# A one-core ViT block on Trainium2: the first projection in high and low parts with its loads split, and three routed tiles picked from parts that GpSimd makes

## The reference

```python
h = tok(x, W, b, cls_token, pos_enc)          # patches @ W.T + b, class token, + pos_enc
h = h + attn(layernorm(h), ...)               # a * cumsum(K @ W) @ U.T, Z terms, @ Wo.T
h = h + ffn(layernorm(h), ...)

logits = xf @ w_router + b_router
topv, topi = top_k(softmax(logits), 2)
pos = cumsum(one_hot(e_flat, 8), axis=0)[arange(n * 2), e_flat] - 1
keep = pos < cap                              # cap = 185
buf = zeros((8, cap, d)).at[e_flat, posc].add(where(keep, xf[tok], 0))
hid = gelu(einsum('ecd,edf->ecf', buf, w1) + b1)
out = einsum('ecf,efd->ecd', hid, w2) + b2
# every token gets back the weighted mean of its kept experts' rows
```

## Time and profile before

| | us |
|---|---|
| median of 3 runs | 159.71 |
| lowest and highest | 159.04, 161.41 |
| profiled execution, first to last instruction (span) | 157.9 |
| PE busy in it | 148.0 |
| DVE, ACT, POOL busy in it | 105.5, 82.8, 50.9 |

### The profile page before, as it was taken

How to read it: one execution, slowest core, us unless ns; L and a number is a source line. 1 busy time by engine, 2 the same in 40 slices (tenths; PEclk the granted TensorE clock), 3 DMA queues, 4 the chain that set the end, 5 groups by cost and what they waited for, 6 DMA issues and landing times.

```text
span 157.9 us, 2961 instructions
## 1 busy us (share of the span) xinstructions
PE 148.0 (94%) x982; PEld 138.4 (88%) x982; DVE 105.5 (67%) x330; ACT 82.8 (52%) x210; POOL 50.9 (32%) x55
## 2 busy tenths in 40 slices
PE   7999999999999979999999999999999999999950
PEld 6548999899789768899799899999999999999940
DVE  0074994769887898981396859669486694785710
ACT  3222754644317998857066557474682665737100
POOL 6001200505530000005437167084371661604361
PEclk9999999999999999999999999999999999999995
DMA  5999960079000345301499897888868978600422
GB/s 169 406 420 435 394 230 0 0 243 338 5 0 22 138 163 184 116 0 28 97 349 292 272 269 194 269 192 307 269 130 270 262 250 264 131 7 0 48 25 23
DMA packets 16978, 28.46 MB, mean 180 GB/s; under 512 B 1133, under 2 KB 13591, under 8 KB 16585
## 3 DMA queue, kind: packets, MB, share of 16 engines
q1 hardware_dynamic: 14505, 25.49, 46.6%
q0 software_dynamic: 2464, 2.86, 10.6%
HBM read 24.21 MB, written 4.14 MB: 180 GB/s over the span
## 4 chain that ended last, share of the span: by engine, by line
PE 65%; DMA 11%; DVE 7%; ACT 6%; issue 3%; POOL 3%; SPq 1%; POOLq 1%; DVEq 0%
PE ps L1298 20%; PE ps L1333 10%; PE ps L1132 6%; PE ps L1223 6%; DMA w_even<-w 5%; DMA first_t<-first 4%; PE ps L1335 4%; PE ps L1240 3%; ACT xn L556 2%; PE ps L1165 2%; PE ps L1343 2%; PE ps L1310 2%; DMA rows_in<-xrows,src_row 2%; PE ps L1261 2%; ACT xn L565 2%
## 5 line engine op out<-in xcount | busy, mean ns | idle before, releaser
L497 POOL DMA_INDIRECT out_rows<-out_s,dst_row x16 | 23.8, 1485 | 38.4 <-ACT out_s L682 32.1
L658 ACT ACTIVATE first_t<-ps,b_cur 128x186 f32<-128x186 f32 x64 | 23.0, 413 | 23.5 <-PE ps L1298 22.0
L1333 PE MATMUL ps<-hid_hl,split 128*128 128x372 f32 x96 | 29.1, 369 | 0.0
L1335 PE MATMUL ps<-hid_hl,split 128*128 128x186 f32 x96 | 23.9, 249 | 0.0
L1298 PE MATMUL ps<-first_t,patch_t 128*128 128x186 f32 x128 | 21.7, 322 | 0.1
L977 DVE CAST hid_hl<-first_t 128x372 fp32r<-128x372 f32 x28 | 10.7, 383 | 15.9 <-ACT first_t L658 15.9
L1298 PEld LDWEIGHTS ps<-first_t,patch_t 128*128 128x128 f32 x128 | 20.1, 190 | 0.4 <-issue 0.4
L482 POOL DMA_INDIRECT rows_in<-xrows,src_row x14 | 15.6, 1113 | 11.0 <-DVE src_row L945 7.1
L1298 PE MATMUL ps<-first_t,w_even 128*128 128x186 f32 x112 | 18.9, 321 | 0.0
L522 ACT ACTIVATE split<-patch_t 128x512 fp32r<-128x512 f32 (+2 forms) x28 | 14.4, 577 | 8.1 <-DMA patch_t<-patches 5.7
L1335 PEld LDWEIGHTS ps<-hid_hl,split 128*128 128x128 f32 x96 | 18.3, 191 | 0.0
(11 more groups left out here) (179 smaller groups left out, 263.2 us busy)
## 6 DMA issues: line engine op xcount, KB each, us to landing
w_even<-w SPq DMA_DIRECT2D x8, 1024.0 KB, 5.7
patch_t<-w SPq DMA_DIRECT2D x8, 1024.0 KB, 5.5
att<-attn SPq DMA_DIRECT2D x1, 1280.0 KB, 9.4
patch_t<-patches SPq DMA_DIRECT2D x1, 1188.0 KB, 14.0
patch_t<-patches SPq DMA_DIRECT2D x1, 1080.0 KB, 11.5
first_t<-first SPq DMA_DIRECT2D x1, 978.0 KB, 7.0
out_rows<-h SPq DMA_DIRECT2D x2, 384.0 KB, 2.5
xrows<-xn SPq DMA_DIRECT2D x2, 384.0 KB, 3.5
```

Source lines behind the costliest of these rows:

```text
L497: pool.indirect_dma_start(out=out[:, :], out_offset=bass.IndirectOffsetOnAxis(ap=dst_row[0:SIZES[s], c:c + 1], axis=0), in_=out_s[q][0:SIZ ...
L658: ins = act.activation(hid[:, f, :], bank(pair)[:, (f % 2) * SL:(f % 2 + 1) * SL], ACT.Gelu, bias=b1_cur[q][:, f:f + 1])
L1333: pe.matmul(dst[:, 0:2 * SL], w2_h[q][:, f, cols], hid_hl[:, f].rearrange("p a s -> p (a s)"), start=f == 0, stop=False)
L1335: ins = pe.matmul(dst[:, 0:SL], w2_l[q][:, f, cols], hid_hl[:, f, 0], start=False, stop=f == KF - 1)
```

## The change

- The first projection's loads are six, one for each slice, with `vecs` behind the second. Slices 0 and 1 stay plain fp32; for 2 to 5 ACT makes high parts of weights and patches and DVE the low parts, and PE makes three f32r products of each, the high product of a slice ahead of the low ones of the slice before.
- `att` is loaded in two pieces: output matrices (384 KB) in front of the second projection's patches, the rest behind. Unit `mac` moves behind the second projection, and its steps on ACT too; `m_high` now stands in front of `xn_high`.
- The rows of tiles 6, 7 and 8 are split by POOL into f32r parts; their one-hots are written as f32r; PE picks them by two f32r products (high and low) for each half. Tile 9 is picked before them. `keep2` of group E moves in front of `rows2` of C.
- POOL makes `at_p` for tiles 7 and 8, the product with the tiles' first rows, and the product with the first part of the weights. DVE keeps the rest.
- `look_up` stands in front of the last up pair of expert 0 instead of behind it. ACT loads the Gelu table behind the half copy.

```diff
+PICK_PARTED = (6, 7, 8)
+PLACES = [*range(6), 9, *PICK_PARTED]
+BY_POOL = (7, 8)
...
-PIECES = [(0, 1), (1, 3), (3, KP)]
+PLAIN = 2
...
-        UNITS = [("proj", A, 0), ("mac", 0, 2), ("uw", 0, 1), ("norm1", A, 0), ("proj", B_, 3), ("norm1", B_, 3),
+        UNITS = [("proj", A, 0), ("uw", 0, 2), ("norm1", A, 0), ("proj", B_, 3), ("mac", 0, 1), ("norm1", B_, 3),
...
-        ACT_ORDER = [("mac", 0), ("root1", A), ("norm1", A), ("xn_high", A), ("m_high", 0), ("root1", B_), ("norm1", B_),
+        ACT_ORDER = [("root1", A), ("norm1", A), ("mac", 0), ("m_high", 0), ("xn_high", A), ("root1", B_), ("norm1", B_),
...
-                     ("rows2", B_), ("squares2", C), ("root2", C), ("rows2", C), ("keep2", E), ("rows2", E), ("keep2", C)]
+                     ("rows2", B_), ("squares2", C), ("root2", C), ("keep2", E), ("rows2", C), ("rows2", E), ("keep2", C)]
...
-            for i, (a, b) in enumerate(PIECES):
+            for k in range(KP):
                 w = D + FIRST
-                sp.dma_start(first_t[:, a:b].rearrange("p k d -> p (k d)"), first[:, a * w:b * w]).then_inc(first_in[i], 16)
-            sp.dma_start(vecs[:, :], vectors).then_inc(vec_in, 16)
-            sp.dma_start(att[:, :], attn).then_inc(attn_in, 16)
+                sp.dma_start(first_t[:, k], first[:, k * w:(k + 1) * w]).then_inc(first_in[k], 16)
+                if k == PLAIN - 1:
+                    sp.dma_start(vecs[:, :], vectors).then_inc(vec_in, 16)
+            sp.dma_start(att[:, 0:A_U.stop], attn[:, 0:A_U.stop]).then_inc(uw_in, 16)
             for g in range(1, len(PATCHES)):
                 c0, c1 = patch_cols(g)
                 sp.dma_start(patch_t[:, c0:c1], patches[:, c0:c1]).then_inc(patch_in[g], 16)
                 if g == 1:
+                    sp.dma_start(att[:, A_U.stop:], attn[:, A_U.stop:]).then_inc(attn_in, 16)
                     sp.dma_start(cst[:, :], const).then_inc(const_in, 16)
...
+            for i, t in enumerate(PICK_PARTED):
+                if t == GROUPS[C][0]:
+                    pool.wait_ge(row_made, 1)
+                elif t < GROUPS[E][0]:
+                    done(pool, ("rows2", C))
+                else:
+                    pool.wait_ge(row_made, 2)
+                pool.tensor_copy(pick_h[:, i], xn[:, t]).then_inc(row_high, 1)
+                pool.wait_ge(row_high, i + 1)
+                pool.tensor_tensor(pick_l[:, i], xn[:, t], pick_h[:, i], ALU.subtract).then_inc(row_split, 1)
+
+            pool.wait_ge(slots_fixed, 1)
+            for t in BY_POOL:
+                for k in range(2):
+                    pool.tensor_scalar(at_p[:, t, k], iota_slot[:, 0:ST], slot_p[:, t, k:k + 1], None, ALU.is_equal
+                                       ).then_inc(pool_marked, 1)
+            pool.wait_ge(places_known, 1)
+            for c in range(1, ID_SUM):
+                start = ids.rearrange("p (t c a b) -> p t c a b", c=ID_SUM, a=1, b=1)[:, :, c]
+                pool.tensor_tensor(marks[:, :, :, 1 + c], at_q, start.broadcast_to((TT, NT, 2, SC)), ALU.mult
+                                   ).then_inc(pool_marked, 1)
+            pool.wait_ge(first_part, 1)
+            pool.tensor_tensor(marks[:, :, :, ID_PARTS], at_q, spread(parts[:, :, :, 0], NT, SC), ALU.mult
+                               ).then_inc(pool_marked, 1)
+
...
-            for i, (a, b) in enumerate(PIECES):
-                act.wait_ge(first_in[i], 16)
-                copy(tok_h[:, a:b], tok_wt[:, a:b]).then_inc(tok_high, 1)
+            for k in range(PLAIN, KP):
+                act.wait_ge(first_in[k], 16)
+                copy(tok_h[:, k], tok_wt[:, k])
+                copy(patch_h[:, k, 0:FIRST], first_t[:, k, D:]).then_inc(first_high, 1)
+            for k in range(PLAIN):
+                act.wait_ge(first_in[k], 16)
+            copy(tok_h[:, 0:PLAIN], tok_wt[:, 0:PLAIN]).then_inc(tok_high, 1)
...
+            patches_high(SPLIT[1], inside=INSIDE + 1)
...
-                    patches_high(SPLIT[1], inside=INSIDE + 1)
...
-            act.activation(idle[:, :], eps_col[0:1], ACT.Gelu)
-
             act.wait_ge(picked, KD)
             copy(buf_t[0][:, 1:], pick_slot[:, 1:]).then_inc(half_ready, 1)
+
+            act.activation(idle[:, :], eps_col[0:1], ACT.Gelu)
...
-            for i, (a, b) in enumerate(PIECES):
-                dve.wait_ge(tok_high, i + 1)
-                dve.tensor_tensor(tok_l[:, a:b], tok_wt[:, a:b], tok_h[:, a:b], ALU.subtract).then_inc(tok_split, 1)
+            for k in range(PLAIN, KP):
+                dve.wait_ge(first_high, k - PLAIN + 1)
+                dve.tensor_tensor(patch_l[:, k, 0:FIRST], first_t[:, k, D:], patch_h[:, k, 0:FIRST], ALU.subtract)
+                dve.tensor_tensor(tok_l[:, k], tok_wt[:, k], tok_h[:, k], ALU.subtract).then_inc(first_split, 1)
+            dve.wait_ge(tok_high, 1)
+            dve.tensor_tensor(tok_l[:, 0:PLAIN], tok_wt[:, 0:PLAIN], tok_h[:, 0:PLAIN], ALU.subtract).then_inc(tok_split, 1)
...
-                for t in range(t0, t0 + n):
-                    dve.tensor_scalar(onehot[:, t], iota_slot[:, 1:SL + 1], place0[:, t:t + 1], None, ALU.is_equal
+                for t in PLACES[t0:t0 + n]:
+                    dst = onehot_r[:, PICK_PARTED.index(t)] if t in PICK_PARTED else onehot[:, t]
+                    dve.tensor_scalar(dst, iota_slot[:, 1:SL + 1], place0[:, t:t + 1], None, ALU.is_equal
...
-            n = marked(dve.tensor_tensor(slot_p[:, :, :], slot_p[:, :, :], lost[:, :, :], ALU.add))
+            dve.tensor_tensor(slot_p[:, :, :], slot_p[:, :, :], lost[:, :, :], ALU.add).then_inc(slots_fixed, 1)
             behind(m)
             m = marked(dve.tensor_tensor(got[:, :], weight[:, :, 0], weight[:, :, 1], ALU.add))
-            behind(n)
+            dve.wait_ge(slots_fixed, 1)
             dve.tensor_tensor(at_q[:, :, :, :], grid(iota_slot[:, 0:SC], NT, 2, SC), spread(slot_q[:, :, :], NT, SC), ALU.is_equal
                               ).then_inc(places_known, 1)
             behind(m)
             m = marked(dve.scalar_tensor_tensor(got[:, :], every[:, :], 1e-6, got[:, :], ALU.mult, ALU.max))
             take_in(0, 0, first=True)
-            find_slots(0, 2)
+            find_slots(0, 1)
             behind(m)
             m = marked(dve.reciprocal(got[:, :], got[:, :]))
-            dve.wait_ge(places_known, 1)
-            for c in range(1, ID_SUM):
-                start = ids.rearrange("p (t c a b) -> p t c a b", c=ID_SUM, a=1, b=1)[:, :, c]
-                dve.tensor_tensor(marks[:, :, :, 1 + c], at_q, start.broadcast_to((TT, NT, 2, SC)), ALU.mult)
...
+            dve.tensor_copy(parts[:, :, :, 0], weight[:, :, :]).then_inc(first_part, 1)
...
             m = rest_after(1)
-            find_slots(7, 9)
+            find_slots(6, BY_POOL[0])
             behind(m)
             m = part_of(2)
-            find_slots(9, NT)
+            find_slots(BY_POOL[-1] + 1, NT)
             behind(m)
-            for k in range(2):
-                ins = dve.tensor_tensor(marks[:, :, k, ID_PARTS:],
-                                        at_q[:, :, k].rearrange("p t (a q) -> p t a q", a=1).broadcast_to((TT, NT, PARTS, SC)),
-                                        parts[:, :, k].rearrange("p t (c a) -> p t c a", a=1).broadcast_to((TT, NT, PARTS, SC)),
-                                        ALU.mult)
+            dve.wait_ge(places_known, 1)
+            for c in range(1, PARTS):
+                ins = dve.tensor_tensor(marks[:, :, :, ID_PARTS + c], at_q, spread(parts[:, :, :, c], NT, SC), ALU.mult)
             ins.then_inc(marks_ready, 1)
...
+                pe.wait_ge(pool_marked, 2 * len(BY_POOL) + ID_SUM)
...
-                pick_tiles(range(t0 - HELD, t0), range(KD))
-                for k in range(KD):
-                    pick_tiles(range(t0, t0 + c), [k]).then_inc(picked, 1)
+                pick_tiles([*range(t0 - HELD, t0), *(t for t in PLACES[t0:] if t not in PICK_PARTED)], range(KD))
+                for i, t in enumerate(PICK_PARTED):
+                    pe.wait_ge(onehot_ready, PLACES.index(t) + 1)
+                    pe.wait_ge(row_high, i + 1)
+                    for k in range(KD):
+                        pe.matmul(pick_slot[:, k, :], pick_h[:, i, k * 128:(k + 1) * 128], onehot_r[:, i, :],
+                                  start=False, stop=False)
+                    pe.wait_ge(row_split, i + 1)
+                    for k in range(KD):
+                        ins = pe.matmul(pick_slot[:, k, :], pick_l[:, i, k * 128:(k + 1) * 128], onehot_r[:, i, :],
+                                        start=False, stop=t == PICK_PARTED[-1])
+                        if t == PICK_PARTED[-1]:
+                            ins.then_inc(picked, 1)
...
-                        for i, (a, b) in enumerate(PIECES):
-                            pe.wait_ge(first_in[i], 16)
-                            for d in range(KD):
-                                for k in range(a, b):
```

(32 more changed lines are left out.)

43 lines of the change are left out of this document (24 added, 19 removed).

## The result

The changed kernel took **161.79 us** (median of 4 runs, 160.66 to 162.31), the kernel before beside it 159.38 (4 runs): a ratio of 1.0145, 95% interval 1.0104 to 1.0186. That is 2.4 us slower in the medians (2.3 by the ratio), where 0.8 us faster was forecast; the time lies above the range given (157.4 to 161.3). The profiled execution had a span of 160.1 us, against 157.9 before.

The account below looks back on a forecast made before the run. PE, busy 94% of the span, was taken as the bound, with DVE's serial chain deciding in the routing. Terms -1.1 - 0.25 - 0.4 + 1.0 = -0.75 us gave span 157.15; plus 1.8, rounded to 158.9 us, range 157.4 to 161.3.

Parts of the forecast that it names:

- the front: First projection through second: split loads and f32r slices gain 1.1 us, moved `mac` and earlier `m_high` 0.25; shift 1.35.
- POOL beside DVE: Routing: POOL's added operations hold up DVE's short steps in three waits of 0.33 us, 1.0 us lost.
- rival 2: Routing, `is_one` to `marks`: POOL holds up DVE throughout, 2.0 us before the copy, 1.3 at look-up; 161.2 us, chance 0.25.
- Marks and look-up: Expert 0's look-up: marks 1.05 us earlier if POOL costs nothing; look-up loses nothing, earlier row numbers and loads gain 0.4.
- `m_l` wait: PE's 0.26 us wait for POOL at 31.62 goes, as ACT runs `m_high` before `xn_high`; gain 0.25 us.
- Picks: Routing, three tiles in f32r: 0.7 us less PE work, counted at nothing because PE is not late there.
- The clock: Clock falling in PE's longer gap, together with rival 2, was the only way above 162.9 us; chance 0.05.

Follow-up runs that it names:

- bystander: Kernel before with spare products, plus POOL's three copies and three subtractions, whose results nothing reads; half copies wait for the last: 160.92 us, ratio 1.0091.
- changed kernel with spare products: Changed kernel plus products nobody reads, filling PE's two gaps ahead of the first pick: 161.73 us, ratio 1.0138.
- control: Kernel before plus products nobody reads, filling PE's two gaps ahead of the first pick: 159.82 us, ratio 1.0013.
- front bridged: Kernel before with only the changed front, plus unread spare products in PE's two gaps ahead of the first pick: 159.91 us, ratio 1.0035.
- Picks back: Changed kernel with all picks in fp32 again and POOL's six splitting steps out; marks shared, look-up early: 161.07 us, ratio 1.0076.
- routing-only: Kernel before with only the changed picks, marks and look-up; front as before: 161.97 us, ratio 1.0123.
- only the marks shared: Changed kernel with spare products, look-up late, picks in fp32 without POOL's six steps; POOL keeps its share of marks: 159.94 us, ratio 1.0016.
- the look-up early: Kernel before with spare products, only the look-up moved one up pair earlier, nothing on POOL: 160.15 us, ratio 1.0027.

## Why the prediction was wrong

By stretches the forecast was -1.35 for the front, +1.0 up to the first up product and -0.4 behind it; the traces show -0.47, +1.51 and +1.23. The differences are 0.9, 0.5 and 1.6 us; of the 0.5, some 0.3 us is the clock's fall in that trace.

**POOL beside DVE** was sized right up to the copy: 1.0 us forecast, 0.95 to 0.99 in the traces of bystander and changed kernel with spare products, in three waits, as forecast. Which three was partly wrong. `is_one` was named and waited, `chosen` hardly did (0.27), and `at_q` took 0.49 us as before; the others were `below` and the one-hots, which the forecast had at its upper end only. The one-hots are of a kind that the rows had not shown, with a single large operand in SBUF: 1.47 us for four against 1.00. The Trainium skill (SBUF — State Buffer, section "SBUF: two separate sides") has it that a DVE operation in a 2-port mode is locked out by a GpSimd one too. The traces show the one-hots held, as that would have it, but not in which mode they ran. The price of rival 2, 2.0 us before the copy, did not come; its side of the result did.

**The step that failed is "Marks and look-up"**, forecast as nothing lost and 0.4 us gained. It took the marks to be ready 1.05 us earlier, less two waits, because DVE had less to do. They were ready 71.66 - 66.50 = 5.16 us after the copy, before 70.46 - 65.47 = 4.99: no earlier at all. POOL's `at_p` took 0.66 us each, not 0.25, so its two products came late, at 68.67 and 69.36, onto DVE's last steps, 0.89 instead of 0.35 and 0.70 instead of 0.17. PE then stood 0.70 us. The 0.4 us counted as a gain for earlier row numbers became a loss of 0.66. The row numbers did let expert 2's first matrix be issued 0.37 us earlier against the first up product (11.11 us behind it, 11.48 before), but the load in the chain of waits is the second matrix, which also waits for the end of expert 0 on PE: it started 12.60 us behind the first up product instead of 12.08, and took 8.33 us instead of 7.57, the latter for reasons that stay open. With the look-up moved back both losses went in the traces, 1.17 us in the medians. So the step is wrong by 1.6 us in all, twice the net gain that was forecast.

**The front** was mis-sized: 1.35 us forecast, 0.47 at `slots` (0). The first projection ended at 12.64, not 11.85, because ACT got its slices at 6.41 and 8.61 and PE's eight plain records took 0.55 us each instead of the 0.355 reckoned with, and the second projection started at 14.60, not 13.95; the patches came at 13.04, not 12.45. Of the `m_l` wait of 0.26 us, DVE's `h_t` gave 0.18 back. The baseline also varies: the control's trace has the same fp32 projection ending at 3.86 + 8.51 = 12.37, with no wait for a load, 0.6 us earlier than in the trace from which the gain was reckoned. In three other traces these 24 records, with no wait either, took 9.53 to 9.91 us and ended at 13.44 to 13.64. So not only loads vary there but PE's records. With the split front the first projection ended at 12.29 to 12.64 in seven of nine traces, and later (13.53 and 15.83) where ACT had its slices late. By these traces the split front is worth about 1 us where PE's early fp32 records are slow, and nothing where they are quick; in the medians nothing is left: front bridged 159.91, control 159.82.

**Picks**: counted at nothing, and that held. With the spare products PE stood 1.32 us for the copy in the changed kernel, where it stood 0.26 in the control.

**The clock** had 0.05 as a cause beyond rival 2. It fell, and in that trace the stretch to the first up is 0.30 us longer than without it (10.53 against 10.23). Taking the fall away left the time where it was: the table under "Picks back" shows that PE's slow pick and DVE's waits for POOL lie in the same microseconds, so that the fall adds 0.35 us where it costs 1.23 alone. That holds for a fall of this length; the one in the routing-only trace was twice as long and cost more.

## What to carry to other kernels

Before work goes to GpSimd beside VectorE's chain of short steps, add the same steps as bystanders whose results nobody reads: that gives their price at this place, here 1.1 us for six steps that save PE nothing. If the clock falls in some executions, compare like with like: here a fall hid most of what taking the steps away gave. Do not move a consumer earlier on the strength of work taken from its producer until a trace shows the producer done earlier, and look for every condition of a load before counting on its earlier start. And reckon a gain at the start from several traces, since the same fp32 projection ended at 12.37 to 13.64 us in five of them.

## What the runs showed of the hardware

- POOL's comparison of 96 elements per partition, written as bf16, took 0.66 us each (0.64 with only the marks shared), its cast of 256 fp32 elements 0.39 us. DVE was busy throughout the comparisons, so this may hold waiting.
- DVE's steps did not stretch beside POOL's casts as they did beside its subtractions: `chosen`, beside a cast, 0.27 us against 0.19.
- PE's granted clock fell at about 58 us after PE had been busy 0.47 and 0.37 us of the two microseconds before. The kernel before had nearly the same idle times there, 0.30 and 0.86 us, and fell in 24 of 84 executions; without the further spare products the kernels with the split front did so in 24 of 31, with them all kernels together in 13 of 91. Why the front matters for a fall 40 us later is open.
- PE's early fp32 records of 396 columns varied: 24 of them took 8.51 us in the control and 9.91 with the look-up early, neither with a wait for a load. In the changed kernel's trace they began at 4.61, 5.27 and 5.93, 0.66 us apart, where 0.33 to 0.36 is usual later. The profile prints a granted clock of 1.00 for both; what slows them is open.
